# First stage of a graph network and expert layer on one core: norm and weight halves first, block ranks beneath the products, second weights' products in the counting, one-hot rows in a ring of three pairs

## The reference, cut to what matters

```python
h = (x @ W.T).reshape(n, heads, out_ch)              # x: the normed nodes, 1250 x 768; W1: 1024 x 768
a_src = jnp.einsum('nhc,hc->nh', h, att_src)
a_dst = jnp.einsum('nhc,hc->nh', h, att_dst)
e = jax.nn.leaky_relu(a_src[src] + a_dst[dst], NEG_SLOPE)
ex = jnp.exp(e - m[dst])
denom = jax.ops.segment_sum(ex, dst, num_segments=n)
out = jax.ops.segment_sum((ex / denom[dst])[:, :, None] * h[src], dst, num_segments=n)
```

## Time and profile before

| | |
|---|---|
| median of 3 executions | 1865.25 us (1864.38 to 1867.32) |
| the profiled execution | 1863.45 us, span 1861.6 us |
| PE busy | 1716.4 us, 92% of the span |
| DVE, ACT, POOL busy | 1116.8, 857.5, 266.1 us |
| mean granted clock of PE | 0.982 |

### The profile page before, as it was taken

How to read it: one execution, slowest core, us unless ns; L and a number is a source line. 1 busy time by engine, 2 the same in 40 slices (tenths; PEclk the granted TensorE clock), 3 DMA queues, 4 the chain that set the end, 5 groups by cost and what they waited for, 6 DMA issues and landing times. The chain is left out here.

```text
span 1861.6 us, 30086 instructions
## 1 busy us (share of the span) xinstructions
PE 1716.4 (92%) x9905; PEld 998.0 (54%) x9905; DVE 1116.8 (60%) x1768; ACT 857.5 (46%) x1358; POOL 266.1 (14%) x116
## 2 busy tenths in 40 slices
PE   3998999779999979989998999999999968999999
PEld 1444444356556546545553555555556545666555
DVE  7997777679999945443222455555555555665301
ACT  2247888688888835421111333333333325555200
POOL 1000000088878805000000000000000000000000
PEclk9999999979999999999999999999999998999999
DMA  6100000011222132030100221111111215440121
GB/s 241 26 1 0 30 0 1 0 25 33 35 48 32 19 82 71 2 126 35 35 26 17 85 67 67 67 67 67 67 67 67 67 73 179 163 145 28 54 68 49
DMA packets 49619, 108.41 MB, mean 58 GB/s; under 512 B 16526, under 2 KB 18664, under 8 KB 49420
## 3 DMA queue, kind: packets, MB, share of 16 engines
q1 hardware_dynamic: 49484, 107.38, 18.8%
q10 hardware_dynamic: 64, 0.08, 0.0%
HBM read 79.02 MB, written 28.43 MB: 58 GB/s over the span
## 5 line engine op out<-in xcount | busy, mean ns | idle before, releaser
L838 POOL TENSOR_TENSOR base<-s_row,ln_c 128x1250 f32<-128x1250 f32 x80 | 227.5, 2845 | 54.5 <-DVE top L893 53.1
L737 PE MATMUL fs<-one_src,one_dst 128*128 x1062 | 211.9, 346 | 23.7 <-ACT one_dst L665 13.7
L93 PE MATMUL di_l<-x2t_hi,ph_hi 128*128 128x512 f16 (+1 forms) x576 | 195.7, 340 | 5.2 <-POOL p L1455 3.8
L94 PE MATMUL di_l<-x2t_lo,ph_hi 128*128 128x512 f16 (+1 forms) x576 | 195.7, 340 | 0.0
L95 PE MATMUL di_l<-x2t_hi,ph_lo 128*128 128x512 f16 (+1 forms) x576 | 195.7, 340 | 0.0
L597 DVE TENSOR_SCALAR one_src<-iota,src 128x1280 f16 x354 | 171.5, 549 | 38.5 <-PE fs L737 31.6
L962 PE MATMUL at_o<-pt,h 128*128 128x384 f32 (+1 forms) x480 | 185.0, 523 | 0.0
L737 PEld LDWEIGHTS fs<-one_src,one_dst 128*128 x1062 | 102.5, 97 | 132.4 <-issue 105.3
L949 PE MATMUL at_t<-ident,q 128*128 128x128 f32 x800 | 107.7, 284 | 29.2 <-ACT q L872 28.5
L93 PE MATMUL co_c<-ps_hi,hid_hi 128*128 128x305 f16 (+1 forms) x384 | 115.5, 301 | 20.8 <-DVE ps_lo L1757 20.1
L949 PEld LDWEIGHTS at_t<-ident,q 128*128 128x128 f32 x800 | 92.5, 145 | 73.8 <-ACT q L872 64.8
(11 more groups left out here) (252 smaller groups left out, 3271.4 us busy)
## 6 DMA issues: line engine op xcount, KB each, us to landing
logits_t<-lg SPq DMA_DIRECT2D x32, 625.0 KB, 3.7
logits_in<-logits_t SPq DMA_DIRECT2D x32, 625.0 KB, 4.6
phf<-in_phi SPq DMA_DIRECT2D x32, 384.0 KB, 3.9
s_row<-a_rows SPq DMA_DIRECT2D x9, 640.0 KB, 6.0
ew1f<-in_fw SPq DMA_DIRECT2D x6, 768.0 KB, 5.1
wf<-in_fw SPq DMA_DIRECT2D x12, 384.0 KB, 5.2
xs<-in_x SPq DMA_DIRECT2D x10, 384.0 KB, 4.3
res<-in_x SPq DMA_DIRECT2D x10, 384.0 KB, 3.0
```

The costliest lines, as they stand in the source:

```text
L93: eng.matmul(out, lh, rh, start=first, stop=False, skip_group_check=True)
L94: eng.matmul(out, lh, rl, start=False, stop=False, skip_group_check=True)
L737: mm = eng.matmul(counts(j)[:, a:a + n], one_dst[:, ds(slot(pair, m) + i, 1), :], one_src[:, ds(slot(pair, m) + i, 1), a:a + n], start=Fal ...
L838: eng.tensor_tensor(base[:, k % 2, 0:N], s_row[:, head % 2, 0:N], ln_c[:, j, 0:N], ALU.add)\
```

## The change

In the order of the diff: the one-hot rings hold three pairs (18 columns) in place of four blocks, slots go by thirds of a ring, and the ring's first third lies where W1's low halves end, so only two pairs can be built before the products end. `apart` holds two pairs. The second layer's weights come one eighth at a time into one buffer, after the products. The pieces of W1 are issued without waiting for each other. `ranks_of_tiles` is cut into `tiles_of_edges`, `ranks_of_blocks` and `farthest_ranks`, and these, `nodes_of_edges`, `farthest` and `bounds_of_tiles` move beneath the tiles 0 to 8 of the products. VectorE starts with the first two tiles' statistics and norms, then W1's low halves. In the loop `weigh(t-1)` now stands ahead of `norm(t+2)`. `second_weights` moves behind the counting loops 1 to 8. The one-hot rows are 1250 wide, not 1280. ScalarE makes the destinations' rows for a pair at once, with one wait for a free pair, and TensorE waits once a pair for them. The closing matmuls have 2 columns. A first small matmul frees two pairs as the program starts, the one after the products a third.

```diff
@@ -277,33 +277,37 @@
...
-    XS, XT, BLOCKS, PAIR = 4, 3, 4, 2
+    XS, XT, RING, PAIR = 4, 3, 3, 2
+    GROUP = PAIR * BLOCK
...
+    early_at = early.at
...
+    early_end = early.at
...
+    early.at = early_at
+    attb = early("attb", [P, 2, D], F32)
+    w2f = early("w2f", [P, D], F32)
+    early.at = early_end
...
-    lns = mem("lns", [P, 2, NP], F32)
...
-    mem.at = after_wt
-    w2f = mem("w2f", [P, KC, D], F32)
-    attb = mem("attb", [P, 2, D], F32)
-    after_w2 = mem.at
-    mem.at = after_wt
-    one_src = mem("one_src", [P, BLOCKS * BLOCK, NP], F16)
...
+    lns = mem("lns", [P, NP], F32)
...
+    mem.at = after_wt - GROUP * NP * 2
+    one_src = mem("one_src", [P, RING * GROUP, NP], F16)
+    after_one = mem.at
...
-    mem.at = after_w2
...
+    mem.at = after_one
...
@@ -326,12 +330,13 @@
...
-    one_dst = mem("one_dst", [P, BLOCKS * BLOCK, P], F16)
-    apart = mem("apart", [P, PAIR, BLOCK, P], F16)
+    one_dst = mem("one_dst", [P, RING * GROUP, P], F16)
+    apart = mem("apart", [P, 2, GROUP, P], F16)
...
@@ -378,7 +383,9 @@
...
-            return (pair % 2) * PAIR * BLOCK + n * BLOCK
...
+            return ((pair + 1) % RING) * GROUP + n * BLOCK
...
@@ -399,24 +406,31 @@
             load_x(1)
             stored_w1 = w1t.rearrange("(k p) c -> p k c", p=P)
             for k in range(KD):
-                if k:
-                    eng.wait_ge(in_w1, 16 * k)
-                eng.dma_start(w1f[:, k, :], stored_w1[:, k, :]).then_inc(in_w1, 16)
+                eng.dma_start(w1f[:, k, :], stored_w1[:, k, :]).then_inc(in_w1[k], 16)
             load_x(2)
             load_x(3)
             eng.dma_start(att[:, :, :], att1.unsqueeze(0).to_broadcast([P, 2, C1])).then_inc(in_att, 16)
-            eng.wait_ge(prep, 5)
-            eng.dma_start(attb[:, :, :], att2.unsqueeze(0).to_broadcast([P, 2, D])).then_inc(in_w2[0], 16)
-            eng.dma_start(w2f[:, :, :], w2t.rearrange("(k p) c -> p k c", p=P)).then_inc(in_w2[1], 16)
             for t in range(XS, NT):
                 load_x(t)
             eng.dma_start(bias_col[:, :], bias.rearrange("o (h c) -> (o c) h", h=HEADS),
                           allow_slow_non_contiguous=True).then_inc(in_bias, 16)
+            def load_w2(k):
+                if k:
+                    eng.wait_ge(v2_ready, 2 * k)
+                eng.dma_start(w2f[:, :], w2t[k * P:(k + 1) * P, :]).then_inc(in_w2f, 16)
+            eng.wait_ge(h_done, NT)
+            eng.dma_start(attb[:, :, :], att2.unsqueeze(0).to_broadcast([P, 2, D])).then_inc(in_attb, 16)
+            load_w2(0)
+            load_w2(1)
             eng.wait_ge(a_kept, 1)
             eng.dma_start(a_rows, a_turned[:, :]).then_inc(stored, 16)
             eng.wait_ge(stored, 16)
             load_s(0)
             load_s(1)
+            for k in range(2, KC):
+                load_w2(k)
         @block.gpsimd
         def _(eng):
@@ -430,7 +444,9 @@
-            def ranks_of_tiles():
+            full = [P, NT, ET]
+            def tiles_of_edges():
@@ -440,16 +456,17 @@
...
-                full = [P, NT, ET]
...
-                for n, rank in enumerate((up, down)):
-                    eng.wait_ge(prep, 2 * n + 1)
-                    eng.tensor_tensor(ranks[:, :, :], within[:, :, :],
-                                      rank[:, :].unsqueeze(1).to_broadcast(full), ALU.mult).then_inc(prep, 1)
-                    eng.wait_ge(prep, 2 * n + 2)
-                    eng.tensor_reduce(ends[:, n * NT:(n + 1) * NT], ranks[:, :, :], AX_X, ALU.max)\
-                       .then_inc(prep, 1)
...
+            def ranks_of_blocks(n, rank):
+                eng.wait_ge(prep, 2 * n + 1)
+                eng.tensor_tensor(ranks[:, :, :], within[:, :, :],
+                                  rank[:, :].unsqueeze(1).to_broadcast(full), ALU.mult).then_inc(prep, 1)
...
+            def farthest_ranks(n):
+                eng.wait_ge(prep, 2 * n + 2)
+                eng.tensor_reduce(ends[:, n * NT:(n + 1) * NT], ranks[:, :, :], AX_X, ALU.max).then_inc(prep, 1)
...
@@ -538,12 +555,12 @@
...
-                    for i in range(2):
-                        eng.wait_ge(in_w2[i], 16)
+                    eng.wait_ge(in_attb, 16)
+                eng.wait_ge(in_w2f, 16 * (k + 1))
...
-                    eng.tensor_tensor_reduce(unread[:, n, :], w2f[:, k, :], attb[:, n, :], 1.0, 0.0,
+                    eng.tensor_tensor_reduce(unread[:, n, :], w2f[:, :], attb[:, n, :], 1.0, 0.0,
...
@@ -556,37 +573,48 @@
             def finish(j):
                 eng.wait_ge(ln_ready, j + 1)
-                eng.scalar_tensor_tensor(ln_c[:, j, :], lns[:, j % 2, :], NONE_TIMES, lns[:, j % 2, :],
+                eng.scalar_tensor_tensor(ln_c[:, j, :], lns[:, :], NONE_TIMES, lns[:, :],
                                          ALU.mult, ALU.min).then_inc(out_ready, 1)
-            ranks_of_tiles()
-            moments(0)
-            moments(1)
-            nodes_of_edges()
-            norm(0)
-            farthest()
-            norm(1)
-            for k in range(KD):
+            def low_w1(k):
                 eng.wait_ge(wt_hi, k + 1)
                 eng.scalar_tensor_tensor(wt[1][:, k, :], w1f[:, k, :], S_WEIGHT, wt[0][:, k, :],
                                          ALU.mult, ALU.subtract).then_inc(wt_lo, 1)
-                if k == 1:
-                    low_x(0)
-                if k == 3:
-                    bounds_of_tiles()
+            moments(0)
+            norm(0)
+            moments(1)
+            norm(1)
+            low_w1(0)
+            low_x(0)
+            for k in range(1, KD):
+                low_w1(k)
             moments(2)
             for t in range(NT):
                 if t + 1 < NT:
                     low_x(t + 1)
+                if t >= 1:
+                    weigh(t - 1)
                 if t + 2 < NT:
                     norm(t + 2)
                 if t + 3 < NT:
                     moments(t + 3)
-                if t >= 1:
-                    weigh(t - 1)
-                if 1 <= t <= KC:
-                    second_weights(t - 1)
-            eng.wait_ge(v2_ready, 2 * KC)
+                if t == 0:
+                    tiles_of_edges()
+                elif t == 1:
+                    ranks_of_blocks(0, up)
+                elif t == 2:
+                    farthest_ranks(0)
+                elif t == 3:
+                    ranks_of_blocks(1, down)
+                elif t == 4:
+                    farthest_ranks(1)
+                elif t == 5:
+                    nodes_of_edges()
+                elif t == 6:
+                    farthest()
+                elif t == 8:
+                    bounds_of_tiles()
             for j, first, last, shift in spans(eng, True):
                 with eng.Fori(first, last) as pair:
@@ -594,12 +622,14 @@
                         eng.wait_ge(free, PAIR * pair + n + 1)
                         at = block_columns(PAIR * pair + n, shift)
                         for i in range(BLOCK):
-                            eng.tensor_scalar(one_src[:, ds(slot(pair, n) + i, 1), :], const["iota"][:, :],
+                            eng.tensor_scalar(one_src[:, ds(slot(pair, n) + i, 1), 0:N], const["iota"][:, 0:N],
                                               src[:, ds(at + i, 1)], None, ALU.is_equal).then_inc(src_ready, 1)
                 if j == 0:
                     weigh(NT - 1)
                     logits()
-                if j == 1:
+                if 1 <= j <= KC:
+                    second_weights(j - 1)
+                if j == KC + 1:
                     eng.wait_ge(v2_hi, 1)
                     eng.scalar_tensor_tensor(v2[1][:, :, :], v2f[:, :, :], S_TURN, v2[0][:, :, :],
                                              ALU.mult, ALU.subtract).then_inc(v2_lo, 1)
@@ -631,17 +661,17 @@
...
-                if j >= 2:
-                    eng.wait_ge(out_ready, j - 1)
-                eng.activation(lns[:, j % 2, :], counts(j)[:, 0:NP], ACT.Ln, bias=const["none"][:, 0:1], scale=2.0)\
+                if j >= 1:
+                    eng.wait_ge(out_ready, j)
+                eng.activation(lns[:, :], counts(j)[:, 0:NP], ACT.Ln, bias=const["none"][:, 0:1], scale=2.0)\
...
-                eng.wait_ge(in_w1, 16 * (k + 1))
+                eng.wait_ge(in_w1[k], 16)
...
-                if k == 1:
+                if k == 0:
...
@@ -655,18 +685,20 @@
             for j, first, last, shift in spans(eng, True):
                 with eng.Fori(first, last) as pair:
+                    eng.wait_ge(free, PAIR * pair + PAIR)
                     for n in range(PAIR):
-                        eng.wait_ge(free, PAIR * pair + n + 1)
                         at = block_columns(PAIR * pair + n, shift)
                         for i in range(BLOCK):
-                            eng.activation(apart[:, n, i, :], const["iota"][:, j * P:(j + 1) * P],
+                            eng.activation(apart[:, ds(pair % 2, 1), n * BLOCK + i, :],
```

(61 more changed lines are left out.)

## The result

The changed kernel takes 1844.18 us (median of 4, 1842.16 to 1846.05) against 1865.24 for the one before, measured beside it: ratio 0.9885, 95% interval [0.9868, 0.9902], 21.1 us faster. The forecast was 1852.8 with a range down to 1845.0: the sign is right, the gain is 21 instead of 12. The profiled execution took 1844.12 us (span 1842.3).

A forecast was written before the change was run, and what follows sets the result against it. TensorE and VectorE were taken to bound the products, TensorE's instruction queue the counting. Terms -7.6 - 2.6 - 1.7 - 0.5 = -12.4 from 1865.25 gave 1852.8 us; own range 1849 to 1856, 8 in 10 range 1845 to 1859.

The forecast's parts named there:

- Start of the products: First product at 16.65 us, the start 15.1 forward; last weight piece lands at 17.5, nothing waits for a load.
- VectorE beneath the products: Some 18.5 us of moved work makes VectorE lag and TensorE stand for norms; TensorE the bound again from tile 6.
- Rival 1: Ranks fit beneath the products, TensorE loses no time there; -18.5 by VectorE's own sum, 1847 us; chance 0.13.
- The second road of rival 4: VectorE's one-hot rows of 1250 take 0.71 us, a pair about 4.4, +24 us; chance 0.04.
- The clock charge of 1.7: Half clock behind TensorE's first stop beneath the products costs 1.7 us: products end at 114.0, not 112.3.
- Head start and first border: Pairs built before the last product ends: counting starts at 114.5, -7.6; three pairs in the ring at first border: -2.6.
- TensorE's queue: In the counting, one wait instruction of 34 ns less per pair, 59 pairs: -1.7 us, bounds -5.5 and +5.7.
- the bound that I had written, 0.09: Counting gains 0.09 us a pair, -5.5 in all, if the removed wait costs as much as a long fused instruction.
- Closing matmuls: Closing matmuls of 2 columns: 0 for nine borders between counts, -0.5 us at the end of the counting.

The follow-up runs named there:

- the chained run: Changed kernel with the six loads of the first weights issued one after the other again, each when the one before has landed: 1864.27 us, ratio 0.9926.
- without the head start: Changed kernel with no pair of one-hot rows built before the last product has ended: 1849.37 us, ratio 0.9917.
- The program with both edits: Changed kernel with VectorE's norms ahead of the logits and one wait a pair for the one-hot rows: 1852.42 us (ratio 0.9862), again 1847.18 (0.9839).
- The one with the norms alone: Changed kernel with VectorE's norm of t+2 and moments of t+3 ahead of the logits of t-1: 1855.11 us (ratio 0.9869), again 1852.28 (0.9869).

## Why the prediction was right in sign and wrong in size

**Start of the products: right.** First product at 16.54 (forecast 16.65), last piece of weights at 17.8 (17.5). That nothing waits for a load was right but for 0.19 on ScalarE, and the chained run shows what hangs on it: without that line of the change 10.85 of the stage's 20.86 would be gone. The text gave it no price. That the rest of the earlier start comes from moving the ranks is read from the two traces; no run puts them back in front.

**VectorE beneath the products: right in kind, 1.3 too long.** It is the bound to tile 5, and TensorE stands for norms behind logits, each in the forecast place. VectorE ends tiles at 30.21, 39.46, 50.38, 59.62 and 70.54, 0.8 to 1.3 ahead of the forecast: the edges' tiles took 4.17 from start to start and not 4.4, a rank step 1.71 and a reduction 3.39 (50.38 - 46.99) and not 1.88 and 3.53. Rival 1 (all fits beneath) fell: 7.5 us of stops. The second road of rival 4 fell too: a row took 543 ns, and not 0.71 us.

**The clock charge of 1.7: the step that failed in this part.** I took half clock for certain behind the first stop of 2 us, from one row, and charged all of it to the products' end. The changed kernel's three longer stops brought none in either of its profiles (1.70, 2.27 and 2.27 in the first; 2.93, 2.27 and 2.27 in the second, with the same end of the products). Seven profiles have this product stage. In them stops of 2.0 to 2.9 us were followed by a lower clock in 6 of 18 cases: ahead of tile 3's transposes at 36.7 in 2 of 6, ahead of 56.9 in 0 of 5, ahead of 77.0 in 4 of 7. The four profiles with half clock at 77.0 end the products at 111.97 to 112.25, the three without at 110.93 to 111.09, so it costs 1.0 to 1.2 at the end. Two of the four had half clock at 36.7 as well and end no later (111.97 and 112.07): the charge at the first stop, the one that I priced, hid beneath VectorE. Behind the products, where the stops from the last product to the first pair were 2.75 to 4.3 us, half clock came in all three profiles that have such a stop, and without the head start the first count was 0.7 longer, not 1.7; what makes the difference I can't say.

**Head start and first border: right.** The first pair stands 0.60 behind the products and the border gained 2.61. The old counting's own half clock, 0.7 of the first count, was left out of the sum.

**TensorE's queue: the term that was mis-sized, -1.7 for about -6.5** (-5.96 - 1.28, without 0.7 of the clock). I priced a removed wait by the duration of its instruction, 34 ns. The runs put 0.09 a pair on that wait in the old kernel and 0.13 in the new, and 0.09 on a wait of the other kind. And I took the slots' arithmetic as neutral; together with the deeper ring it gave 0.03. For the wait alone the bound that I had written, 0.09, was the value in the old kernel. It should have been the forecast, since the same part says that the queue sets the pair, and the trace had no row for what a wait costs there beyond its duration.

**Closing matmuls: right,** 0 and -0.5.

**The range** ended at 1845.0, just above the result. Products without the charge (112.3) and the queue's bound (-5.5) together would have given 1847.3, and VectorE's 1.3 less makes 1846.0, still inside. What led out of it was left out of the working: the 0.7 of half clock in the old first count, and the 1.0 by which the queue's gain passed its bound. By how little it lies outside is partly luck: the profile has no half clock at 77.0, and with its 1.0 to 1.2 the result would be, as an estimate, at 1845.2 to 1845.4, just inside. The queue would be mis-sized all the same.

## What to carry to other kernels

Where an engine's own instruction queue sets the pace, price an edit by the change of the cadence in a run with that edit alone, not by the removed instruction's duration; one redundant wait cost two and a half times its own duration. When a stage is moved forward, look first at what its start was hiding: here loads chained one after the other had been free, and would have taken half of the gain at the stage's end. And put the work that another engine waits for ahead of the long work that nobody waits for yet: the norms ahead of the logits were worth 2.3 to 2.5 us at the stage's end.

## What the runs showed of the hardware

The clock's fall behind a stop is not settled by the stop's length. The program with both edits had a window of 0.81 over 8 us behind its stop of 2.23 in one profile and 1.00 in the other. The one with the norms alone had 1.00 behind its stop of 2.34 at 55.56 in one, and 0.57 (window 56 to 60) behind the same stop at 55.97 in the other. Behind the first border's stop of 1.51, with a whole pair of rows waited for, it fell to 0.57; behind the 2.27 ahead of 77.0 it stayed in three of seven profiles.

At the very start the matmuls of the first product stand 0.43 us apart until 20.38, twice their later 0.216, which is the level of 1.2 GHz, while the windows give the granted clock as 1.00. The trace's clock records begin only at 20.80, so the 1.00 ahead of them is no measurement. This stretch is no matter of the kernel: the same program had it for 4.3 us in one profile and for 1.7 in the other, the kernel before for 1.7. It left the products' end where it was (110.95 and 110.93), because the stop ahead of tile 3's transposes took it up (1.70 with the long stretch, 2.93 with the short one).

And operand addresses with a remainder by three went with shorter fused instructions (46 ns) than with one by two (51); no run changed that alone.
